# Self-attention on one core: where VectorE takes a turned tile's low part, and in which steps the output weights are split

## The reference

```
qkv    = x @ weight_qkv.T      # 4 groups, each 4 query heads, one key head, one value head of 128
scores = q @ k.T / sqrt(128), masked above the diagonal
attn   = softmax(scores)
out    = (attn @ v), 16 heads side by side, @ weight_proj.T
```

## Time and profile before

| what | value |
|---|---|
| median of 3 runs | 1867.03 us (1865.27 to 1870.76) |
| the profiled execution | 1867.1 us, its span 1865.4 us |
| TensorE busy | 1763.7 us, 95% of the span |
| VectorE busy | 1216.4 us, 65% |
| ScalarE busy | 979.6 us, 53% |
| GpSimd busy | 290.4 us, 16% |
| self-attention in the trace | about 55 to 909 us |
| granted TensorE clock, mean | 0.98 of full speed |

### The profile page before, as it was taken

How to read it: one execution, slowest core, us unless ns; L and a number is a source line. 1 busy time by engine, 2 the same in 40 slices (tenths; PEclk the granted TensorE clock), 3 DMA queues, 4 the chain that set the end, 5 groups by cost and what they waited for, 6 DMA issues and landing times.

```text
span 1865.4 us, 27936 instructions
## 1 busy us (share of the span) xinstructions
PE 1763.7 (95%) x10281; PEld 1360.4 (73%) x10281; DVE 1216.4 (65%) x2477; ACT 979.6 (53%) x2045; POOL 290.4 (16%) x831
## 2 busy tenths in 40 slices
PE   5799999999999999988899999999999999999998
PEld 4688888888888888866544444444389999999997
DVE  6655656566655656566587878879654247667766
ACT  2444444444444444333488888888742136666651
POOL 1000000000000000032145453443111500000015
PEclk9999999999999999998899999999989999999999
DMA  4000000010000000000000007000010448878756
GB/s 147 1 1 12 23 24 1 1 35 1 24 1 21 15 23 1 1 7 6 1 1 7 1 16 259 1 1 1 1 49 38 155 154 289 274 272 304 267 163 226
DMA packets 83942, 131.58 MB, mean 71 GB/s; under 512 B 4832, under 2 KB 47840, under 8 KB 83808
## 3 DMA queue, kind: packets, MB, share of 16 engines
q1 hardware_dynamic: 78688, 113.01, 17.9%
q0 software_dynamic: 5120, 16.78, 2.6%
HBM read 96.75 MB, written 33.03 MB: 70 GB/s over the span
## 4 chain that ended last, share of the span: by engine, by line
PE 81%; DVE 11%; ACT 6%; issue 1%; DMA 0%; POOL 0%; ACTq 0%
PE ps L175 36%; PE ps L181 11%; PE ps L1323 8%; PE ps L1103 7%; PE ps L1206 6%; PE ps L1019 5%; PE ps L1186 4%; DVE xmax L1647 3%; PE ps L1196 2%; ACT xp L1447 2%; DVE nmax L1620 1%; DVE probs L1628 1%; ACT o_t L1454 1%; DVE stats L192 1%; DVE al L1709 1%
## 5 line engine op out<-in xcount | busy, mean ns | idle before, releaser
L1647 DVE TENSOR_REDUCE xmax<-ps 128x1 f32<-128x512 f32 x512 | 324.8, 684 | 71.8 <-PE ps L1186 70.0
L1447 ACT ACTIVATE xp<-ps 128x512 f32<-128x512 f32 x512 | 281.0, 611 | 56.4 <-PE ps L1196 56.3
L1383 ACT ACTIVATE probs<-ps,nmax 128x128 f32<-128x128 f32 (+3 forms) x256 | 136.2, 532 | 168.3 <-DVE nmax L1620 168.2
L1196 PE MATMUL ps<-q3m,k 64*128 64x512 f32 x512 | 192.5, 452 | 2.1 <-ACT xp L1447 2.1
L1186 PE MATMUL ps<-k,q 64*128 64x512 f32 x496 | 190.2, 452 | 3.2 <-DVE xmax L1647 3.1
L1186 PEld LDWEIGHTS ps<-k,q 64*128 64x128 f32 x496 | 78.5, 184 | 130.0 <-DVE xmax L1647 47.4
L1417 ACT CAST pth<-ps 128x128 fp32r<-128x128 f32 (+3 forms) x256 | 108.5, 424 | 86.6 <-PE ps L181 86.6
L1206 PE MATMUL ps<-xp,vx 128*32 128x512 f32 x1024 | 136.0, 604 | 0.8 <-issue 0.8
L808 POOL TENSOR_TENSOR rstd<-ve,half 128x4 f32<-128x4 f32 x9 | 11.2, 1247 | 803.9 <-DVE ve L203 803.9
L1620 DVE TENSOR_REDUCE nmax<-ps 128x1 f32<-128x128 f32 (+3 forms) x256 | 124.8, 488 | 11.2 <-PE ps L1019 9.8
L1709 DVE TENSOR_TENSOR al<-ps,ah 128x512 fp32r<-128x512 f32 x64 | 44.3, 692 | 128.8 <-ACT ah L1422 128.8
(11 more groups left out here) (193 smaller groups left out, 3998.3 us busy)
## 6 DMA issues: line engine op xcount, KB each, us to landing
w_raw<-in_w_t SPq DMA_DIRECT2D x56, 704.0 KB, 6.2
w_raw<-in_w_t SPq DMA_DIRECT2D x28, 768.0 KB, 5.7
rows_x<-w_raw SPq DMA_DIRECT2D x1, 9984.0 KB, 30.2
mixed<-rows_x SPq DMA_DIRECT2D x39, 256.0 KB, 4.5
rows_y<-y_s SPq DMA_DIRECT2D x39, 256.0 KB, 5.4
w_raw<-in_w_qkv_t SPq DMA_DIRECT2D x24, 256.0 KB, 2.9
res<-in_x SPq DMA_DIRECT2D x4, 1024.0 KB, 8.2
wo_raw<-in_w_proj_t SPq DMA_DIRECT2D x4, 1024.0 KB, 5.4
```

Source lines behind the costliest of these rows:

```text
L1196: pe.matmul(ps[:, XST + BANKS[n], :], k3[half_of(h), kv % 4, t * P:(t + 1) * P], q3m[half_of(h), h // 2, :], start=True, stop=True).then_i ...
L1383: act.activation(probs[u % 4][:, 0:w], ps[:, S_BANK + u % 2, 0:w], ACT.Exp, bias=nmax[:, u % 4:u % 4 + 1], accum_out=rsum[:, u % 4:u % 4 + ...
L1447: act.activation(xp[:, kv % 2, h, t, :], ps[:, XST + BANKS[n], :], ACT.Exp, scale=X_SCALE).then_inc(s_xe, 1)
L1647: dve.tensor_reduce(xmax[:, slot, i, h:h + 1], ps[:, bank, :], AX_X, ALU.max, negate=True).then_inc(s_xmax, 1)
```

## The change

VectorE takes the low part of the tile turned in the step before as its first work in a step that has scores, ahead of the maximum and the weighing, where it came behind both. And the four splits of the output weights go from steps 10, 11, 12 and 13 of a group's first batch to steps 9, 11, 13 and 15, for ScalarE and VectorE alike.

```diff
+SPLIT_OUT = [9, 11, 13, 15]
...
             score, done = b * UNITS + s + 1, b * UNITS + s - 1
             if s < UNITS and score < BATCH * UNITS + (not last):
                 ops.append(("score", score))
-            if b == 0 and 10 <= s < 10 + QPG:
-                ops.append(("split_out", s - 10))
+            if b == 0 and s in SPLIT_OUT:
+                ops.append(("split_out", SPLIT_OUT.index(s)))
...
                     elif op[0] == "first_s":
                         maximum(0, 0, op[1], G_BANK + op[1] % 2)
+                    if op[0] == "score" and lag:
+
+                        for turn in lag:
+                            low_turned(g, *turn)
+                        lag = []
                     if op[0] == "score":
                         maxima(g, op[1])
                     if op[0] == "score" or (op[0] == "turn" and op[1] >= weighed):
```

## The result

The changed kernel took 1856.06 us in the median of nine runs (1845.04 to 1858.21), the kernel before 1871.49 in nine runs beside them: a ratio of 0.9902 with an interval of 0.9876 to 0.9928, some 18 us or 1% faster. The profiled execution took 1845.8 us, its span 1844.1; the profiled one of before took 1867.1 (span 1865.4).

A forecast was written before the change was run, and what follows sets the result against it. TensorE, with 81% of the chain, was taken as the bound, standing for the low part (ptl). 15.7 - 2.2 - 1.2 - 0.7 - 0.8 + 5.7 + 5.6 = 22.1 us off 1867.1 gave 1845.0 us, range 1839 to 1858.

The forecast's parts named there:

- (a): Batch ends: v's transposes start 1.12 us earlier at 14 places, a gain of 15.7 us.
- (b): Transposes of tile 15, awaiting v's low part: no cost at ten batch ends, 0.55 us at four with splits, -2.2 us.
- Rival B: The wait only moves: tile 15's transposes ask back 0.9 us at 14 places, 12.6 us, giving 1857.6 us; chance 0.10.
- (c): Other steps: maximum 1.0 us later in steps 3, 7, 11, 1.4 in 9, 13; slack 0.3 to 0.5 us, no stall.
- (d): Groups' last batches lose 1.2 us together, the first batch's PV of 67.89 0.7, the last group's third batch 0.8.
- Part 2: Output weights' splits moved to steps 9, 11, 13 and 15: 1.4 us gained in four batches, +5.6 us.
- (e): Last batch: PV at 827.05 instead of 830.62, 3.6 us, and two later PVs 1.2 and 0.9 us: +5.7 together.
- rival C: More gain: with less idle time TensorE's clock may stay up, about 5 us, giving 1840 us; chance 0.15.
- Rival A: Little gain in the last group: without the last batch's 5.7 us the kernel takes 1850.7 us; chance 0.17.
- Rival E: Nothing to measure: a wait stands behind the low part that the list puts down to it; chance 0.05.
- Rival D: Slower: the ring laps TensorE at 64 places, 0.5 us each at 0.9 us above the working: +32, 1877; chance 0.05.
- the ring: In the new order maximum, exponential, cast and low part become bound to each other, some 2.3 us round.

The follow-up runs named there:

- e3: Kernel before, with the low part first only in step 14, ahead of the turning of v: 1885.8 us, ratio 0.9908 to the kernel before.
- e6: Changed kernel, with the low part first only in step 14 and in the last batch of all: 1840.7 us, ratio 0.9845 to the kernel before.
- e2: Changed kernel with the low part back behind maximum and weighing, only the splits moved: 1898.0 us, ratio 0.9966 to the kernel before.
- e5: Changed kernel run again unaltered: 1852.6 against 1869.4 us for the kernel before, ratio 0.9915.
- e7: Changed kernel with each of GpSimd's two long memsets cut in four pieces: 1848.1 us, ratio 0.9883 to the kernel before.
- e9: Kernel before with two idle copies on ScalarE ahead of each exponential's wait for its maximum: ratio 1.0001 to the kernel before.
- e1: Changed kernel with the output weights' splits back in steps 10 to 13: 1884.5 against 1903.7 us for the kernel before, ratio 0.9905.
- e10: Changed kernel with the edits of e6 and e7 together: 1872.7 against 1905.6 us for the kernel before, ratio 0.9828.
- e8: Changed kernel with two idle copies on ScalarE ahead of each exponential's wait for its maximum: ratio 0.99 to the kernel before.
- e4: Changed kernel with the old order in the first group's first steps and the last split in step 14: 1877.9 us, ratio 0.986 to the kernel before.

## Why the prediction was right, and where its working wasn't

The forecast was 1845.0 us, the profiled execution it was made against came out at 1845.8, and the median of the nine runs at 1856.1, inside the range. The gain between the medians, 15 to 18 us, is 70 to 83% of the 22.1. That the traces agree to 0.8 us is luck: against the forecast the start is 3.7 us short and the 13 batches 1.7, the last stretch is 2.5 over, and 2.0 came outside the attention, where nothing was forecast.

- **(a) The gain at v: right.** 1.28 us became 0.16 at all 14 places; e3, with this part alone, gives 1.12 for each of 13 batches.
- **(b) What is late next: right in its mechanism, 0.49 for 0.55 us.** Four waits for vl, in the batch after the splits (2.0 us by the list, 2.2 forecast). The ten other batch ends keep 0.1 us or so: a third batch takes 49.83 us after, 49.76 in e6. Rival B would have shown 0.9 there; it didn't come.
- **(c) "Slack is 0.3 to 0.5 us, no stall": half right.** No wait is marked in steps 3 to 13 of a normal batch. But against e6, a group's first batch takes 0.31 us more (50.07 and 49.76), its second 0.74 (50.49 and 49.75, of which 0.49 is vl) and its last 0.47 (50.84 and 50.37, with 0.22 and 0.31 marked before transposes and PV). That is 1.6 us per group with the third batch, where (b) and (d) had 0.95. The small delays were costed at nothing, and moving these steps had no gain to set against them: e3 and e6 show that the order pays in step 14, ahead of the turning of v, and that in the other steps outside the last batch it costs, taken together. They weren't tried one by one.
- **Part 2: right, 1.54 for 1.4 us each** (e2). Some 0.3 of it is given back in the changed kernel, as above, and the new split in step 15 costs what (b) charges for it. Together with (a) to (d) that makes the 13.7 for 15.4 in the 13 batches.
- **(d) The start: this term failed in size.** The forecast was +1.8 us up to the first v (1.1 + 1.4 - 0.7), the profiled execution lost 1.9. The order explains little of it: e5, the same kernel, takes 51.66 us there, a gain of 0.3, and e6, with the old order at the start, takes 52.69. What differs between the two executions of the one kernel is the clock: TensorE's granted clock was 0.76 and 0.82 in the profiled one's two windows from 40 to 80 us, and 0.91 and 0.91 in e5 (before: 0.91 and 1.00; e6: 0.81 and 0.85). The clock isn't all of it: e3 takes 53.76 us at 0.83 and 0.91. The one part that can be compared at like clocks (0.91 from 40 to 60 us in both) came as forecast: counted from the first staged tile, the first PV is at 23.66 us before (67.89) and at 24.26 in e5 (68.46), 0.6 later for 0.7. The gain of 2.5 (1.1 + 1.4) behind it was 0.9 in e5, and how much of that is the clock is not shown. Windows of before, then of after (us, PE PEld DVE ACT POOL busy, clock, DMA, GB/s):

```profile
40.00:60.00 20.00, 10.78 (x63) 9.11 (x62) 16.12 (x42) 7.11 (x16) 1.32 (x1) 0.91 0.00 0
60.00:80.00 20.00, 16.83 (x102) 14.32 (x101) 12.32 (x35) 9.76 (x28) 0.00 (x0) 1.00 0.00 1
```

```profile
40.00:60.00 20.00, 11.80 (x56) 10.12 (x56) 16.07 (x41) 7.38 (x16) 1.32 (x1) 0.76 0.00 0
60.00:80.00 20.00, 16.96 (x86) 14.14 (x85) 10.11 (x28) 7.64 (x23) 0.00 (x0) 0.82 0.00 1
```

  The third batch of the last group lost 0.9 (54.62 to 55.54), forecast 0.8, and 1.65 in e5; e6, with the old order there, has 54.60.

- **(e) The last batch: the sum was too low, 5.7 us for 8.3, and one step of it wrong.** PV after the memset comes 4.15 us earlier counted from v (11.91 before, 7.76 after), forecast 3.6. The term was rightly named: the new order takes the second held weighing, 3.48 us, from the front of the low part (e3, with the old order in this batch, has the wait of 6.7 us still).

  But the step "it starts when the block before it ends" was wrong. Counted from v, that block, the first held weighing, ends at 7.67 us in either kernel. The forecast started the low part there and ended it at 8.34. In the trace it starts at 6.65, with the end of its cast, and ends at 7.67 with the weighing; so PV comes 0.6 earlier than forecast. And e7, which takes that hold away, moves PV by 0.35 us alone: behind the hold the cast is next.

  From that PV to the cross-attention it is 79.01 us before and 74.85 after: 4.16, where 2.1 were forecast. The gain lies at the two PVs that were forecast, 1.69 to that of 845.89 and 0.92 to that of 858.48 (2.6 for 2.1), 0.04 to the next, at 872.82, and 1.51 behind it, where the last PV and the output's matmuls stand.

  That last part is the clock, and so rival C is in this: from this last PV to the cross-attention it is 18.65 us before at a granted clock of 0.78, 17.14 after at 0.90, 17.23 in e5 at 0.89, but 19.30 in e7 at 0.75 and 20.12 in e6 at 0.71. The first four matmuls of woh take 1.19 us after for 2.08 before. In e7 the slow part only came later, since the 14.4 us ahead of it are 12.6 there. Both stretches together, from the PV of 858.48 on, are 33.03 us before (32.4 to 33.2 in e2, e3 and e9, with the old order) and 31.48 after (31.2 to 31.9 in the six other traces with the new one, bar e6 with 34.00). So some 1.5 us go with the change, but not in every execution. The stretch that answers to the earlier trace rows had 0.60 before, 0.61 in e5 (849 to 875 us) and in the changed kernel's profiled execution 0.74:

```profile
850.00:876.00 26.00, 19.81 (x69) 12.97 (x70) 17.41 (x41) 6.45 (x18) 4.02 (x17) 0.74 0.00 0
```

  The rows of the last PV's stretch, before and then after:

```profile
891.00:909.60 18.60, 16.45 (x60) 13.04 (x60) 3.46 (x5) 0.59 (x1) 3.40 (x14) 0.78 0.00 1
```

```profile
872.80:890.00 17.20, 15.00 (x61) 12.05 (x61) 3.46 (x5) 0.59 (x1) 3.44 (x14) 0.90 0.00 1
```

- **The rule on ports.** In e7 the low part at 814.00 took its usual 0.69 us while pieces of the memset ran, and the weighing at 815.27 took 0.92, with whole memsets 3.36. The Trainium skill ("SBUF — State Buffer", section "Who interferes with whom") says that a VectorE instruction with at most one SBUF input, outside the modes that take the shared ports, doesn't contend with GpSimd. By that rule these rows come out as they did: they agree.
- **Rival A** (little gain in the last group) is out: 7.4 us came there, 6.3 in e5. **Rival E** (nothing to measure) is out as well, by the ratio and its interval. **Rival D** (the ring as the bound) did not come, but its mechanism is the kernel's: 0.40 us more in the ring costs the changed kernel some 40 us and the kernel before 12. The changed order has used up most of the slack that the old one had, as (c) said in calling it "the narrowest place of the plan". D's price came earlier than D had it: it let the stalls begin at 0.4 us above the working and counted +32 at 0.9, and at 0.40 they cost 40 already, in part at places that it didn't name (tile 15's transposes).

**What stays open.** The medians differ from the traces by 3 to 6 us. The stages behind the attention, whose code is the same in all, vary: from the same transpose of the cross-attention as above to the end of the span the trace of before has 955.8 us, after 954.1, e5 957.9, e6 952.1, e7 958.5. What sets this wasn't tried.

## What to carry to other kernels

Find the one place where the bounding engine stands, and move the work that it waits for there alone: e3 had all of part 1's gain in the 13 batches with one step in 16 moved, and a rule applied in every step gave 5.5 us of it back, some 2 of them in delays too short to be marked. When two engines' queues are tied more closely, measure the slack by loading the ring, and put the load behind the ring's own wait: ahead of it, it measures nothing. And compare distances between like instructions, by kind of batch, rather than spans: in one kernel they repeat to 0.1 us, where its runs differ by 13.

## What was not expected of the hardware

**A held instruction holds the completion of those behind it, not their start.** In the trace of before, VectorE behind the weighing of 823.89:

```profile
824.09 2.29 DVE L1654 TENSOR_TENSOR ptl<-ps,pth 128x384 fp32r<-128x384 f32 x1
824.56 1.82 DVE L1620 TENSOR_REDUCE nmax<-ps 128x1 f32<-128x384 f32 x1
825.02 1.36 DVE L1627 RECIPROCAL rinv<-rsum 128x1 f32<-128x1 f32 x1
```

All three end at 826.38, as the weighing does, and are recorded as started at their usual spacing. So a low part's 2.29 us here need not be its own. The prediction said that only weighings are held, and this row, which it didn't show, seems to speak against it. What speaks for it: in the changed kernel the maximum of 814.61 and the reciprocal of 815.08 have no held weighing in front of them, and took 0.55 and 0.15 us, their usual times, beside the memset of 814.88; and e7's low part took 0.69 beside the pieces. How the engine does it is not shown.

**TensorE's clock at the start differs between executions of like code.** The first sixteen transposes of the staged tiles, ahead of anything that the change touches, take 2.03 us before and 3.42 after; e2, e3 and e5 have 2.03 as well, e1, e6 and e10 3.4 to 3.7. From 40 to 60 us the granted clock was 0.82 to 0.91 in the first kind and 0.74 to 0.81 in the second (2.4 GHz is 1.00, 1.2 GHz half of it); e7 stands outside, with 2.50 us and 0.60. Between two executions of the changed kernel the stretch to the first v differs by 2.2 us (53.83 and 51.66).

**The same kernel takes 1869 to 1872 us on two chips and 1904 to 1906 on a third**: 34 us apart, more than the whole gain. The attention has no part in it: it takes 844.8 us in e5, on a fast one, and 844.5 in e8, on the slow one. Behind it the seven traces of the slow chip have 986 to 991 us, all others 952 to 960. In e1, e2, e4 and e8 TensorE stands 22 to 25 us there in waits for which the profile finds no releaser, where before, after and e5 have 0.8; what ends them is not shown. The ratios of like kernels agree (0.9902 and 0.9915 for the changed one at 1869 to 1872 us, 0.99 on the slow chip for e8, whose copies cost nothing).
